# Two mixture-of-experts stages: from all experts over all tokens to rows sent to their experts' regions in DRAM

## What is computed

```python
def _expert(xf, w1, w3, w2):
    return jax.nn.silu(xf @ w1) * (xf @ w3) @ w2
...
logits = xf @ router_w + router_b
topk_vals, topk_idx = jax.lax.top_k(logits, BEST_K)      # 2 of 8
...
gates = jax.nn.softmax(sparse, axis=-1)
```

## Time and profile before

| | |
|---|---|
| median of 3 runs | 4069.66 us |
| the profiled execution | 4072.66 us |
| its span | 4070.9 us |
| PE busy | 3679.8 us, 90% of the span |
| DVE, ACT, POOL busy | 2724.5, 1789.7, 1377.1 us |
| granted PE clock, mean | 0.971 of full speed |
| moved by DMA | 131.72 MB, mean 32 GB/s |
| DMA issued by POOL | none |

### The profile page before, as it was taken

One profiled execution on the slowest core, in us unless ns is written; L12 is line 12 of the kernel. 1 busy time (PEld: TensorE's weight loads), 2 busy tenths in 40 slices (PEclk: granted clock), 3 DMA queues, 4 the chain that ended last, 5 costly groups with the idle time before them and its releaser, 6 DMA issues. The chain is left out here.

```text
span 4070.9 us, 80068 instructions
## 1 busy us (share of the span) xinstructions
PE 3679.8 (90%) x27516; PEld 2888.3 (71%) x27516; DVE 2724.5 (67%) x5625; ACT 1789.7 (44%) x3205; POOL 1377.1 (34%) x1049
## 2 busy tenths in 40 slices
PE   6998788886999799999967999999999969999999
PEld 4887677776888688888854555555555538888888
DVE  5665677776677466666655777777777746666665
ACT  2444344443455333333324666666666643333333
POOL 2555122221566222222242333333333312222222
PEclk9999899998999799999988999999999979999999
DMA  3000000000000100000004233332324210000000
GB/s 104 0 0 9 7 0 0 0 0 1 1 0 0 39 1 0 0 0 0 0 12 114 73 102 85 86 97 76 105 70 113 73 39 11 10 10 15 10 10 16
DMA packets 92753, 131.72 MB, mean 32 GB/s; under 512 B 9824, under 2 KB 42992, under 8 KB 92672
## 3 DMA queue, kind: packets, MB, share of 16 engines
q1 hardware_dynamic: 90624, 130.13, 11.6%
q10 hardware_dynamic: 2048, 0.53, 0.1%
HBM read 71.38 MB, written 58.72 MB: 32 GB/s over the span
## 5 line engine op out<-in xcount | busy, mean ns | idle before, releaser
L1492 DVE TENSOR_REDUCE neg_max_sb<-s_ps 128x1 f32<-128x512 f32 x1024 | 692.8, 687 | 289.4 <-PE s_ps L1219 268.1
L1382 ACT ACTIVATE prob_sb<-s_ps 128x512 f32<-128x512 f32 x1024 | 602.2, 600 | 391.4 <-PE s_ps L1231 374.1
L850 POOL TENSOR_TENSOR m_act_lo_sb<-m_act_sb,m_act_hi_sb 128x512 fp32r<-128x512 f32 x320 | 413.5, 1292 | 1043.8 <-ACT m_act_hi_sb L816 1043.8
L806 ACT ACTIVATE m_silu_sb<-moe_h_ps 128x512 f32<-128x512 f32 x320 | 191.4, 598 | 968.1 <-PE moe_h_ps L761 968.0
L904 DVE TENSOR_TENSOR m_act_sb<-moe_h_ps,m_silu_sb 128x512 f32<-128x512 f32 x320 | 220.5, 689 | 503.2 <-ACT m_silu_sb L806 473.5
L1139 POOL TENSOR_TENSOR prob_sb<-prob_sb,band_sb 128x520 f32<-128x520 f32 (+1 forms) x256 | 285.0, 1113 | 712.6 <-ACT prob_sb L1382 712.6
L1231 PE MATMUL s_ps<-q_stack_sb,k_stack_sb 128*128 128x512 f32 x1024 | 450.8, 441 | 8.2 <-ACT prob_sb L1382 7.9
L1219 PE MATMUL s_ps<-k_stack_sb,q_stack_sb 96*128 96x512 f32 x1024 | 426.4, 419 | 29.9 <-DMA k_stack_sb<-qk_scratch 19.7
L529 POOL TENSOR_TENSOR f_sq_lo_sb<-f_sq_sb,f_sq_hi_sb 128x512 fp32r<-128x512 f32 x256 | 328.9, 1293 | 350.5 <-ACT f_sq_hi_sb L504 350.4
L916 DVE SCALAR_TENSOR_TENSOR x_resident_sb<-moe_y_ps,gates_sb,x_resident_sb 128x256 f32 (+1 forms) x1024 | 422.4, 474 | 0.5
L779 PE MATMUL moe_y_ps<-w2h_sb,m_act_hi_sb 128*128 128x256 f32 x1280 | 367.1, 287 | 12.3 <-DVE x_resident_sb L916 10.0
(11 more groups left out here) (285 smaller groups left out, 8894.2 us busy)
## 6 DMA issues: line engine op xcount, KB each, us to landing
qk_scratch<-qk_hi_sb SPq DMA_DIRECT2D x128, 256.0 KB
q_stack_sb<-qk_scratch SPq DMA_DIRECT2D x128, 192.0 KB, 4.0
k_stack_sb<-qk_scratch SPq DMA_DIRECT2D x128, 192.0 KB, 4.2
qk_scratch<-qk_lo_sb SPq DMA_DIRECT2D x64, 256.0 KB
x_resident_sb<-x SPq DMA_DIRECT2D x4, 2048.0 KB, 17.8
out<-x_resident_sb SPq DMA_DIRECT2D x16, 512.0 KB
moe_w_values_sb<-routed_w SPq DMA_DIRECT2D x12, 512.0 KB, 6.4
q_stack_sb<-neg_max_t_sb ACTq DMA_DIRECT2D x128, 4.0 KB
```

Of the source, the lines that this page charges most:

```text
L850: nc.gpsimd.tensor_tensor(al[:, slot(e), :], act_f[:, e % 2, :], as_f32(ah[:, slot(e), :]), ALU.subtract).then_inc(low_ready, 1)
L1382: nc.scalar.activation(prob[:, kt % 2, i, :], s2p[i % 2][:, :], ACT.Exp).then_inc(exp_done, 1)
L1492: nc.vector.tensor_reduce(nm[:, g % 2, 2 * (i % 2) + i // 2, qt:qt + 1], s1p[n % 2][:, :], AXIS_X, ALU.max, negate=True).then_inc(max_done, 1)
```

## The change

`moe_stage` becomes four phases, each a block of its own, and all of them written out without hardware loops:

1. `dispatch_phase`: per sequence the transposes, the router, and the two shared experts only. DVE works out for each token and each of its two choices a row number in one of eight regions of a DRAM tensor `expert_rows`, from counts that PE sums over tokens with five small f32 matmuls (`places`). POOL then sends the normalised rows there with 8 indirect DMAs per sequence, each of 128 rows of 1040 bytes: 256 values, the gate, the number of the row where the result goes, and two spare.
2. `table_phase`: which expert each of 39 tiles of 512 slots has, and at which row it begins. 39 is 2 x 8192 / 512 + 7, which is enough for any split over the experts; tiles that no expert needs read rows of zeros and are computed all the same.
3. `expert_phase`: the end of each expert's rows is first filled with zeros by 8 DMAs of ACT. Then each tile is loaded by SP (532 KB), transposed, run through one routed expert, scaled by its gates on ACT, and sent by POOL with 4 indirect DMAs of 128 rows of 1024 bytes into `ranked_rows`, where the first choices of all tokens stand in token order and then the second. The tile's w1 and w3 are copied by DVE into a buffer of their own (4 x 2 x 128 values per partition), since the expert is known only by a register.
4. `combine_phase`: per sequence SP and ACT load one result each (512 KB), POOL adds the two, DVE adds the sum to x; then the statistics (first stage) or the store to `out` (second).

What POOL did per expert, the low part of the product, goes to DVE in both phases.

```diff
-                def body(b, p, before, more):
-                    for e in range(E):
-                        hidden(b, p, e)
-                        if e >= LAG:
-                            output(b, e - LAG)
...
+def dispatch_sizes(tokens):
+    region = tokens + TOKENS
+    tiles = TOP_K * tokens // TOKENS + EXPERTS - 1
+    return region, tiles
...
+        self.rows = nc.dram_tensor("expert_rows", (EXPERTS * region + TOKENS, ROW), F32).ap()
+        self.ranked = nc.dram_tensor("ranked_rows", (TOP_K * tokens + 2 * TOKENS, DM), F32).ap()
...
+        with ExitStack() as inner:
+            dispatch_phase(core, a, name + "_a", scratch, w, rw, (own, rank_no, dest), (seen, earlier, zero), inner)
+        table_phase(core, name + "_t", (own, limit, tile_no), (seen, earlier), tab, tail)
+        with ExitStack() as inner:
+            expert_phase(core, name + "_b", scratch, w, trash, tab, tail, zero, inner)
+        with ExitStack() as inner:
+            combine_phase(core, name + "_c", scratch, inner, out)
...
+            pe.wait_ge(pool_made, 4)
+            transpose(0)
+            for b in range(B):
+                hidden(b, 0)
+                if b:
+                    output(b - 1, 1)
+                hidden(b, 1)
+                if b + 1 < B:
+                    transpose(b + 1)
+                output(b, 0)
+                places(b)
+            output(B - 1, 1)
...
+            x_high(0)
+            second(0)
+            for b in range(B):
+                silu_of(b, 0)
+                high_of(b, 0)
+                silu_of(b, 1)
+                if b + 1 < B:
+                    x_high(b + 1)
+                share_of(b)
+                high_of(b, 1)
+                if b + 1 < B:
+                    second(b + 1)
...
+            for b in range(B):
+                pool.wait_ge(second_ready, b + 1)
+                pool.wait_ge(payload_ready, b + 1)
+                pool.wait_ge(index_ready, b + 1)
+                for r in range(TOP_K):
+                    for t in range(TILES):
+                        nc.gpsimd.indirect_dma_start(
+                            scratch.rows, bass.IndirectOffsetOnAxis(ap=idx[:, b % RB, r, t:t + 1], axis=0),
+                            rows[:, b % RB, r, t, :], None).then_inc(sent[b % RB], 16)
...
+            for b in range(B):
+                product(b, 0)
+                if b:
+                    update(b - 1)
+                take_logits(b)
+                low_of(b, 0)
+                choose(b)
+                if b + 1 < B:
+                    x_low(b + 1)
+                product(b, 1)
+                low_of(b, 1)
+                payload(b)
+                index(b)
+                if b + 2 < B:
+                    normalise(b + 2)
+            update(B - 1)
...
+        def _(sp):
+            for i in range(NT):
+                if i >= XR:
+                    sp.wait_ge(tp_ready, i - XR + 1)
+                    sp.wait_ge(dst_ready, i - XR + 1)
+                if i < EXPERTS:
+                    sp.wait_ge(tail_zeroed[i], 16)
+                row = sp.value_load(tab[0:1, 0, i:i + 1], min_val=0, max_val=EXPERTS * REGION)
+                sp.dma_start(xr[:, i % XR, :, :],
+                             scratch.rows[bass.ds(row, TOKENS), :].rearrange("(t p) d -> p t d", p=P)
+                             ).then_inc(loaded[i % XR], 16)
...
+            transpose(0)
+            last = None
+            for i in range(NT):
+                e = pe.value_load(tab[0:1, 1, i:i + 1], min_val=0, max_val=EXPERTS - 1)
+                pe.wait_ge(xl_ready, i + 1)
+                pe.wait_ge(weights_ready, i + 1)
+                if i >= 2:
+                    pe.wait_ge(silu_ready, i - 1)
+                hidden(i, 0, h1, h1_ready)
+                if i + 1 < NT:
+                    transpose(i + 1)
+                if i >= 2:
+                    pe.wait_ge(act_ready, i - 1)
+                hidden(i, 2, h3, h3_ready)
+                if i:
+                    output(i - 1, last)
+                last = e
+            output(NT - 1, last)
...
+        def _(act):
+            for e in range(EXPERTS):
+                row = act.value_load(tail[0:1, e:e + 1], min_val=0, max_val=EXPERTS * REGION - TOKENS)
+                nc.scalar.dma_start(scratch.rows[bass.ds(row, TOKENS), :].rearrange("(t p) d -> p t d", p=P),
+                                    zero[:, :, :]).then_inc(tail_zeroed[e], 16)
...
+            def scale(i):
+                act.wait_ge(y_ready, i + 1)
+                act.wait_ge(dst_ready, i + 1)
+                if i >= 2:
+                    act.wait_ge(sent[i % 2], PER_SENT * (i // 2))
+                for t in range(TILES):
+                    op = nc.scalar.activation(ys[:, i % 2, t, :], y[:, t, :], ACT.Copy, scale=gate[:, i % META, t:t + 1])
+                op.then_inc(ys_ready, 1)
+
+            x_high(0)
+            for i in range(NT):
+                silu_of(i)
+                if i + 1 < NT:
+                    x_high(i + 1)
+                high_of(i)
+                if i:
+                    scale(i - 1)
+            scale(NT - 1)
...
+        def _(pool):
+            for i in range(NT):
+                pool.wait_ge(ys_ready, i + 1)
+                pool.wait_ge(dst_ready, i + 1)
+                for t in range(TILES):
+                    nc.gpsimd.indirect_dma_start(
+                        scratch.ranked, bass.IndirectOffsetOnAxis(ap=dst[:, i % META, t:t + 1], axis=0),
+                        ys[:, i % 2, t, :], None).then_inc(sent[i % 2], 16)
...
+            def weights(i):
+                if i >= 2:
+                    dve.wait_ge(h3_ready, i - 1)
+                e = dve.value_load(tab[0:1, 1, i:i + 1], min_val=0, max_val=EXPERTS - 1)
+                nc.vector.tensor_copy(wt[:, i % 2, :, :, :], w13[:, :, bass.ds(e * KT, KT), :]).then_inc(weights_ready, 1)
...
+            def place(i):
+                dve.wait_ge(loaded[i % XR], 16 * (i // XR + 1))
+                if i >= META:
+                    dve.wait_ge(sent[i % 2], PER_SENT * ((i - META) // 2 + 1))
+                m = i % META
+                g = xr[:, i % XR, :, GATE_AT]
+                d = xr[:, i % XR, :, DEST_AT]
+                nc.vector.tensor_copy(gate[:, m, :], g)
+                nc.vector.scalar_tensor_tensor(spare[:, m, :], d, 0.0, trash[:, i % 2, :], ALU.is_equal,
+                                               ALU.mult).then_inc(spare_ready, 1)
+                dve.wait_ge(spare_ready, i + 1)
+                nc.vector.scalar_tensor_tensor(dst[:, m, :], d, -1.0, spare[:, m, :], ALU.add,
+                                               ALU.add).then_inc(dst_ready, 1)
...
+            weights(0)
+            x_low(0)
+            place(0)
+            for i in range(NT):
+                if i + 1 < NT:
+                    weights(i + 1)
+                    x_low(i + 1)
+                product(i)
+                if i + 1 < NT:
+                    place(i + 1)
+                low_of(i)
...
+        def load(engine, b, r):
+            if b >= RING:
+                engine.wait_ge(x_done, b - RING + 1)
+            n = r * B * TILES + b * TILES
+            engine.dma_start(yb[:, b % RING, r, :, :], ranked[:, n:n + TILES, :]).then_inc(loaded[b % RING], 16)
...
+        def _(pool):
+            for b in range(B):
+                pool.wait_ge(loaded[b % RING], 32 * (b // RING + 1))
+                nc.gpsimd.tensor_tensor(yb[:, b % RING, 0, :, :], yb[:, b % RING, 0, :, :], yb[:, b % RING, 1, :, :],
+                                        ALU.add).then_inc(summed, 1)
+
+        @block.vector
+        def _(dve):
+            for b in range(B):
+                dve.wait_ge(summed, b + 1)
+                xs = core.x[:, b * TILES:(b + 1) * TILES, :]
+                nc.vector.tensor_tensor(xs, xs, yb[:, b % RING, 0, :, :], ALU.add).then_inc(x_done, 1)
+                if out is None:
+                    stats.take(dve, b, lambda: dve.wait_ge(x_done, b + 1))
```

701 lines of the change are left out of this document (477 added, 224 removed).

## The result

The changed kernel takes 3865.69 us, the median of 4 runs (3860.96 to 3869.15), beside 4070.43 for the kernel before, the median of 4 runs on the same chip (4068.98 to 4072.59). The ratio is 0.9499, with a 95% interval of 0.9487 to 0.9511. The forecast was 3837, 0.7% too low.

What follows compares the result with a forecast made beforehand. PE's work was taken to bound the MoE stages. Dispatch 255, table 8, experts 275, combine 67 and the rest 7 gave 612 us for 734, the second stage 623 for 735: 234 less, 3837 us; range 3700 to 4060.

Steps and rivals of the forecast that it cites:

- the main step: MoE stages: PE runs 71 experts instead of 160, 370 us less per stage, not all gained since PE stops being the bound.
- The sum: Whole kernel: phases add to 612 us for 734 and 623 for 735, 234 less, giving 3839, then 3837.
- c: POOL's time for one indirect DMA, without a row in the trace, taken as 1.3 us.
- Rival 1: Dispatch and experts: POOL's DMAs bind at 2.39 us each and cost more than the matmuls saved; 4259 us, chance 0.19.
- Rival 2: Dispatch and experts: POOL and DVE lock each other out of SBUF, 1.8 us per DMA; 3917 us, chance 0.22.
- Dispatch: 14.5 taken: Dispatch, per sequence: a cycle through router and next low part, longer than PE's 12.6 or DVE's 12.7, 14.5 us with hand-overs.
- a half clock: Long phases: PE's clock taken as unchanged; a clock of a half there was listed as a sign of being wrong.
- Experts: 6.3 taken: Expert phase, per tile: the cycle through ACT and DVE binds, 5.7 us, 6.3 with hand-overs; 275 us for the phase.
- POOL's waits ending on ACT's y: Expert phase: a sign of being right, with an expert phase of 240 to 290 us.
- the head: Start of the expert phase: ACT's eight fills some 17 us, then a cast and a low part, together 21 us.
- Last phase, first stage: Combine: DVE's additions and statistics, 3.9 us a sequence with hand-overs, 67 us with its head.
- The register loads: Expert phase: PE's and DVE's register loads have no row; taken at no cost, 8 us per stage kept for the range.

Runs made afterwards that it cites:

- experiment 3: Every indirect DMA of the expert phase issued twice, eight per tile instead of four, against the changed kernel: 4315.39 us, ratio 1.0595.
- experiment 2: Five buffers instead of three for the loads of the last phase, against the changed kernel: 3868.67 us, ratio 0.9514.
- experiment 5: PE always takes expert 0's w2, without register load or register operand, against the changed kernel: 3862.63 us, ratio 0.9492.
- experiment 7: DVE copies the expert's first weights for the first two tiles only, against the changed kernel: 3867.20 us, ratio 0.9510.

## Why the prediction was right

The sign and the size were right, and so was the main step: 560 us of PE's matmuls are gone, and the time gets only 208 of them, since in most phases something else ends last. The size is in part luck, since the phases' errors went both ways: 6 us too much for dispatch, 16 too little for the experts, 10 too little and 6 too much for the last phases. (The sum itself has a slip: 3839 less 3.0 is 3836 and not 3837.) By its own steps:

- **c, the price of an indirect DMA.** Taken 1.3, measured 1.27, and 1.33 on average in the expert phase with the stretch. Rival 1, POOL as the bound at 2.39, did not happen. The Trainium skill (DMA: Bandwidth & Descriptors, section "Anatomy of one DMA") would give about 2.3 us if the wait for completion held POOL; the row shows 0.97, so it doesn't. At eight per tile (experiment 3) the change is a loss of 6%; a part of that is late posts and not the issue.
- **Rival 2, POOL and DVE locked out of SBUF at c = 1.8.** Its reason is borne out in kind: stretched DMAs stand beside DVE's operations in SBUF, in the last phase DVE's step stands still while POOL adds. Its size is not. The stretch is about 0.4 us, at most 0.55, in 64 of 312 DMAs, nearly one a tile as the sum had it (0.75 there). By the Trainium skill (SBUF — State Buffer, section "SBUF: two separate sides") a DMA beside a DVE copy could take 3.1 us; no indirect DMA of the changed kernel took more than 1.51, beside copies of 0.69.
- **Dispatch: 14.5 taken, 14.4 measured, and not for the reasons given.** The cycle was drawn through the router and the next low part. At the full clock PE is the bound: of 13.3 us it is busy for 12.5, and 0.8 is a wait for that low part. The half clock adds 1.2 us on average; the prediction had kept the clock as it was, and had listed a half clock under what would prove it wrong. Two errors of one size, which is luck.
- **Experts: 6.3 taken, 6.56 measured: the step that failed.** "5.7, with hand-overs of about 0.1 each" was too long: undisturbed tiles take 5.37, since each of these operations begins up to 0.14 us before the row of the one before has ended. ACT's order is what sets these. What came on top, 2.6 us in every second tile, was nowhere in the prediction: it forecast "POOL's waits ending on ACT's y" (they do, 177.5 us), but saw nothing that goes from POOL back to PE. The rest of the phase's 16 us: the head took 15 for 21, the first scaling came 13 after the first matmul where the sum had 5.2, the tiles took 10 more, and from the last scaling's start to the end it took 13 for 9.
- **Last phase, first stage: 77 for 67.** The sum took DVE as the bound, 3.9 us a sequence, which is right, and put its stretch by POOL at nothing. DVE's own work is 3.4 a sequence; held steps make it 4.4 (experiment 2). In the second stage 72 for 78, at 350 GB/s on average as the sum had it.
- **The rest.** The register loads, taken at nothing, cost nothing (PE's in experiment 5, DVE's in 7). Stages 1 and 2 give 102 and 108 less; elsewhere nothing changed but for 3 us less ahead of the first stage and some 5 us more in attention, which makes the 208 of the span.

## What to carry to other kernels

Price an indirect DMA by its issue on POOL (1.27 us for 128 rows here), and check that POOL can rest: in these kernels PE's posts came late wherever POOL was asked for one after the other, long before POOL itself was the bound. When a wait repeats in every second tile, look at which post ended it and when that was recorded, before giving it to the buffers; taking the buffers out of question took one run. And judge a deeper ring by the end of the phase and not by the engine that it serves: here POOL's additions came 12 us sooner and the phase ended 5 us sooner, because DVE behind them hardly ever waited.

## What the runs showed of the hardware that I had not expected

- PE's posts come 0.01 us after their matmuls in most of the kernel. Where POOL issues indirect DMAs back to back half of those of y come late, by 3.7 us in the median (36 of 72), and with twice as many 44 of 65, by 13. With two per tile, or with one direct DMA of the same 524 KB (0.75 us of POOL), none is late. In the expert phases no post of ACT or DVE is late in any of these kernels.
- An indirect DMA takes 0.97 us of POOL, and in the changed kernel up to 1.51 beside DVE's operations from SBUF to SBUF. SP's issue of a load takes 0.37 us in every case in the kernel without indirect DMAs in the phase, and up to 0.73 with them, mostly while none of them stands on POOL (12 of 17 in experiment 7).
- The granted clock falls to a half for 10.2 us in the middle of a phase in which PE is busy for 94%, 2 to 5 times a stage, and not at the same places from kernel to kernel; with PE's gap filled (98%) it stays full for 157 and 171 us and then falls too.
- In the last phase DVE's 128x8 step of 0.17 us takes up to 2.2, until POOL's addition ends, and DVE's own addition 3.4 for 1.2 (experiment 2).
